# A score pair, the weighted sum, the other score pair: another order of TensorE's work in each unit of an attention kernel

## The chip, the cores and the metric

One NeuronCore of a Trainium2 chip runs the whole kernel. The metric is the device time of one execution in microseconds (us), as the median of several runs. PE is TensorE, ACT ScalarE, DVE VectorE, POOL GpSimd, SP the engine that issues the DMAs.

## The reference

A block of adaptive layer norm, differential attention and a ternary feed-forward product, for four sequences of 2048 tokens with 256 features. There are 16 heads, each with two softmax maps over a head size of 8:

```python
h = _layernorm(x, axis=-1) * (1 + ca) + sa
# attention of h
q, k = h Wq, h Wk     as 32 half-heads of 8;   v = h Wv  as 16 heads of 16
attn_w = softmax(q k^T * 8 ** -0.5)
aw = attn_w[:, :, 0] - lam * attn_w[:, :, 1]
attn = aw v;  attn = attn * rsqrt(mean(attn ** 2) + 1e-5) * subln_w * (1 - LAMBDA_INIT)
x = x + ga * (attn Wo)
h = _layernorm(x, axis=-1) * (1 + cb) + sb
x = x + gb * (h (ternary(Wf) * scale))
```

The scores are 4 x 32 matrices of 2048 x 2048, and each entry goes through an exponential once.

## The kernel before

**Tiling.** The batches b run from 0 to 3 (B = 4). A batch has 8 groups of two heads; two groups make a body, so there are 4 bodies per batch (index `gp`) and 16 in all. A body has 128 units (`BODY`). A unit is one group, one chunk of 512 queries and one block of 128 keys. Sixteen units with the same queries are a segment.

**Score pairs.** `scores(body, u, n)` (L670) makes one score pair: two bf16 matmuls of 64 rows by 128 columns with 512 moving columns, one on the upper and one on the lower half of the array, both at a time, into two PSUM banks. There are three such slots of two banks (`SLOTS`), used in turn; score pair n waits until the exponential of pair n - 3 is done (`exp_done`). Each unit has two score pairs, 2u and 2u + 1.

**Exponentials.** ACT takes the pairs in order (L576): one activation of 128 x 1024 elements from PSUM to `probs`, a ring of four units.

**Weighted sum.** `weighted(body, u)` (L680) multiplies the exponentials of a unit with the values: four float32 matmuls of 128 x 32 side by side with 512 columns, accumulated in the bank `pv` over the 16 units of a segment. It is made two units late (`LAG`). It waits for the exponentials of its own unit, and in the first unit of a segment also for `pv_read`: DVE must have transposed the last segment's sum out of `pv` (L948). DVE then finishes the segment (`segment`, L941), with POOL's power function in the middle (L549).

**Steps.** Into the units are woven the projections of the next batch (steps 0 to 7: two of transpositions, L596, then queries, keys and values, L610 and L602, in the bodies of batches 0 to 2) and the outputs of the batch before (steps 8 to 13: two of the product with Wo, two of transpositions, two of the feed-forward product, in the bodies of batches 1 to 3). Each step is cut into four pieces of float32 matmuls on tiles of 128 x 32, with 256 columns (in all 8 matmuls a piece in the trace) or, for transpositions, 128. A table places them: of the 16 units of a segment, the pieces stand in units 3 to 6 and 11 to 14 (step 0 in 7 to 10):

```python
STEP_PIECES = {NB * (n // 2) + ((7 if n == 0 else 3), 11)[n % 2] + p: (n, p)
               for n in range(A_STEPS + E_STEPS) for p in range(PIECES)}
```

The first piece of step 0 waits for DVE's normed tile (`a_normed`, L825), whose statistics DVE starts behind the last segment of the body before. In the last body of batches 0 to 2, eleven units also carry a part of the maxima that shift the exponentials (`m_step`, L652).

**Order.** Everything on PE stands in one hand-written loop over the units (L747). Each engine runs its own list in order; a wait holds up what stands behind it on that engine.

Of the kernel before, what the change touches and what calls it, by code (L numbers as in the profile page):

```python
# [15 lines left out]
def wait_alone(eng, sem, value, passed):  # L16

    eng.wait_ge(sem, value)
    eng.sem_inc(passed, 1)  # L20
# [17 lines left out]
def adaln_diff_attention(nc, x, wqT, wkT, wvT, woT, lq1, lk1, lq2, lk2, subln, wfT, cT, wmod, out):  # L38
# [11 lines left out]
    PAIRS = 2  # L50
# [60 lines left out]
    with ExitStack() as ctx:  # L111
# [95 lines left out]
        def slot_of(body, n):  # L207
            return (body * 2 * BODY + n) % SLOTS
# [371 lines left out]
        def _(pe):  # L580
# [89 lines left out]
            def scores(body, u, n):  # L670

                buf, tc, blk = u // UNITS, u // NB % NC, u % NB
                pe.wait_ge(exp_done, body * (2 * BODY) + n + 1)
                for half in range(2):
                    at = 64 * half
                    last = nc.tensor.matmul(slots[slot_of(body, n)][:, half, :], keys[buf][at:at + KS_ROWS, n % PAIRS, blk * P:(blk + 1) * P],  # L676
                                            queries[buf][at:at + KS_ROWS, n % PAIRS, tc * CH:(tc + 1) * CH], start=True, stop=True)
                last.then_inc(scores_ready, 1)

            def weighted(body, u):  # L680

                buf, blk, seg = u // UNITS, u % NB, u // NB
                if blk == 0:
                    pe.wait_ge(pv_read, body * SEGS + seg + 1)
                pe.wait_ge(exp_done, SLOTS + body * (2 * BODY) + PAIRS * (u + 1))
                for pair in range(PAIRS):
                    for half in range(2):
                        j = 32 * (2 * pair + half)
                        last = nc.tensor.matmul(pv[j:j + VW, :], values[buf][:, blk, half, :], probs[:, u % PRING, pair, half, :],  # L689
                                                start=(blk == 0), stop=(blk == NB - 1))  # L690
                last.then_inc(pv_done, 1)
# [19 lines left out]
            for b in range(B):  # L711
                pe.wait_ge(m_flag_set, b + 1)
                exact = pe.value_load(m_flag[0:1, 0:1], min_val=0, max_val=1)
                pe.reg_mov(behind, 1)
                with pe.If(exact > 0):

                    if b > 0:
                        for u in range(BODY - LAG, BODY):
                            weighted(b * GP - 1, u)
                    pe.reg_mov(behind, 0)  # L720

                    runs = pe.snap(exact_runs, min_val=0, max_val=B - 1)
                    pe.wait_ge(m_evacuated, (b + 1) * M_STEPS)
                    pe.wait_ge(pv_read, b * (GP * SEGS) + 1)
                    with pe.Fori(0, NG) as g:
                        pe.wait_ge(m_rows_loaded, (runs * EXACT_LOADS + (g + 1) * ROW_LOADS) * DMA)
                        for n in range(4 * NB):
                            head, blk = n // NB, n % NB
                            pair, at = head // 2, 64 * (head % 2)
                            pe.wait_ge(m_reduced, (runs * NG + g) * (4 * NB) + n + 1)  # L730
                            for k in range(NC):
                                last = nc.tensor.matmul(ps[:, 4 * (n % 2) + k, :], queries[0][at:at + KQ, pair, blk * P:(blk + 1) * P],
                                                        keys[0][at:at + KQ, pair, k * CH:(k + 1) * CH], start=True, stop=True)
                            last.then_inc(m_scores, 1)
                    wait_alone(pe, m_reduced, (runs + 1) * NG * (4 * NB) + 2, pe_passed)
                    for k in range(NC):
                        if k > 0:
                            pe.wait_ge(exact_evacuated, runs * NC + k)
                        m_transposes(k).then_inc(exact_product, 1)
                    wait_alone(pe, exact_evacuated, (runs + 1) * NC, pe_passed)  # L740
                    wait_alone(pe, m_rows_loaded, (runs + 1) * (EXACT_LOADS * DMA), pe_passed)
                    pe.reg_add(exact_runs, exact_runs, 1)

                for gp in range(GP):
                    body = b * GP + gp
                    steps, outputs, maxima = b < B - 1, b > 0, b < B - 1 and gp == GP - 1
                    for u in range(BODY):  # L747
                        if u % UNITS == 0:
                            buf = u // UNITS
                            pe.wait_ge(group_loaded[buf], (body + 1) * (GROUP_LOADS * DMA))  # L750
                        for n in (PAIRS * u, PAIRS * u + 1):
                            scores(body, u, n)
                        if u >= LAG:
                            weighted(body, u - LAG)
                        elif gp > 0:
                            weighted(body - 1, BODY - LAG + u)
                        elif b > 0:
                            with pe.If(pe.snap(behind, min_val=0, max_val=1) > 0):
                                weighted(body - 1, BODY - LAG + u)
                        before = aux_before(b, gp, u, steps, outputs, maxima)  # L760
                        if maxima and u in M_UNITS:
                            i = M_UNITS[u]
                            if before[0] == "a":
                                pe.wait_ge(a_evacuated, (body + NC) * A_STEPS + before[1] + 1)
                            elif before[0] == "e":
                                pe.wait_ge(e_evacuated, (body - GP) * E_STEPS + before[1] + 1)
                            if i > 0:
                                pe.wait_ge(m_evacuated, (b + 1) * M_STEPS + i)
                            m_step(b + 1, i)
                        if u in STEP_PIECES:  # L770
                            n, p = STEP_PIECES[u]
                            if (steps if n < A_STEPS else outputs):
                                if p == 0 and before is not None:
                                    if before[0] == "a":
                                        pe.wait_ge(a_evacuated, (body + NC) * A_STEPS + before[1] + 1)
                                    elif before[0] == "e":
                                        pe.wait_ge(e_evacuated, (body - GP) * E_STEPS + before[1] + 1)
                                    else:
                                        pe.wait_ge(m_evacuated, (b + 1) * M_STEPS + before[1] + 1)
                                if n < A_STEPS:  # L780
                                    if n == 0 and p == 0:
                                        pe.wait_ge(a_normed, body + NC + 1)
                                    elif n == 2 and p == 0:
                                        pe.wait_ge(a_evacuated, (body + NC) * A_STEPS + 2)
                                    last = a_piece(n, p, aux)
                                    if p == PIECES - 1:
                                        last.then_inc(a_product, 1)
                                else:
                                    i = n - A_STEPS
                                    if i == 0 and p == 0:  # L790
                                        pe.wait_ge(e_evacuated, (body - GP) * E_STEPS)
                                        pe.wait_ge(e_loaded, (body - GP + 1) * 3 * DMA)
                                    elif i == 2 and p == 0:
                                        pe.wait_ge(e_normed, body - GP + 1)
                                    elif i == 4 and p == 0:
                                        pe.wait_ge(e_evacuated, (body - GP) * E_STEPS + 4)
                                    last = e_piece(i, p, aux)
                                    if p == PIECES - 1:
                                        last.then_inc(e_product, 1)
# [316 lines left out]
```

## Time and profile before

| | us |
|---|---|
| median of 3 runs (lowest, highest) | 4042.49 (4041.13, 4048.74) |
| the profiled execution | 4045.13 |
| its span, first to last instruction | 4043.3 |
| ACT busy | 3783.7 (94%) |
| PE busy | 3753.5 (93%) |
| DVE busy | 1197.4 (30%) |
| POOL busy | 634.0 (16%) |

A busy share is the time in which the engine has at least one instruction in work, over the span. Matmuls overlap in PE's pipeline and their ends are modelled, so PE's pace is better read from the distances between starts than from busy time.
### The profile page before, as it was taken

The numbers are of one execution on the slowest core, as the hardware profiler recorded it, in microseconds if no ns is written. First come the engines' busy times: TensorE is split into PE (matmuls) and PEld (weight loads), VectorE is DVE, ScalarE is ACT, GpSimd is POOL, SyncE is SP. The second block draws the span as 40 slices with busy tenths as digits, with TensorE's granted clock in tenths as the row PEclk, the third lists the DMA queues.
The fourth block names the chain that finished last, engine by engine and source line by source line (L and its number), as shares of the span: only waits on it lengthen the run. The fifth ranks groups of instructions, "written<-read, shape, count | busy, mean of one in ns | idle before, by whom it ended". The sixth has DMA issues, their size and how long they took to land.

```text
span 4043.3 us, 75625 instructions
## 1 busy us (share of the span) xinstructions
PE 3753.5 (93%) x32082; PEld 919.2 (23%) x32082; DVE 1197.4 (30%) x2826; ACT 3783.7 (94%) x4132; POOL 634.0 (16%) x401
## 2 busy tenths in 40 slices
PE   6699999999999999999989999999999999999996
PEld 3121212222122222222222222222221212222123
DVE  7322222223332322323423223232331212212124
ACT  1599999999999999999989999999999999999992
POOL 4111212111120210202012121211211010101000
PEclk8799999999999999999999999999999999999998
DMA  3302112210231313113130221313012121201202
GB/s 125 88 25 36 41 34 36 37 36 25 34 54 35 53 32 48 39 35 50 35 56 25 40 49 35 54 35 49 29 34 38 24 40 16 49 3 30 35 13 62
DMA packets 112430, 163.26 MB, mean 40 GB/s; under 512 B 18820, under 2 KB 86660, under 8 KB 111880
## 3 DMA queue, kind: packets, MB, share of 16 engines
q1 hardware_dynamic: 112072, 158.19, 20.6%
q8 instruction: 261, 4.28, 0.5%
q14 instruction: 97, 0.79, 0.1%
HBM read 97.82 MB, written 60.32 MB: 39 GB/s over the span
## 4 chain that ended last, share of the span: by engine, by line
ACT 62%; issue 19%; PE 11%; DVE 5%; POOL 2%; SPq 1%; DMA 1%; DVEq 0%; POOLq 0%; ACTq 0%
ACT probs L576 61%; PE ps L689 5%; PE ps L676 3%; PE ps L602 1%; DVE stats L814 1%; POOL seg_rs L549 1%; DVE normed L825 1%; PE ps L596 1%; DVE seg_t L948 1%; POOL a_rest L522 0%; POOL a_parts L524 0%; SPq L316 0%; POOL e_rstd L529 0%; DVE e_tmp L934 0%; DMA m_scr<-wmod_sb 0%
## 5 line engine op out<-in xcount | busy, mean ns | idle before, releaser
L576 ACT ACTIVATE probs<-ps 128x1024 f32<-128x1024 f32 x4096 | 3763.0, 1291 | 87.6 <-PE ps L676 86.0
L689 PE MATMUL ps<-probs,values 128*32 128x512 f32 x16384 | 2193.3, 607 | 26.3 <-DVE seg_t L948 16.9
L676 PE MATMUL ps<-queries,keys 64*128 64x512 bf16 x8192 | 1441.9, 386 | 152.6 <-DMA queries<-m_scr 24.7
L549 POOL TENSOR_TENSOR seg_rs<-seg_ms,neg_half 64x16 f32<-64x16 f32 x128 | 370.2, 2892 | 2582.1 <-DVE seg_ms L957 2582.1
L676 PEld LDWEIGHTS ps<-queries,keys 64*128 64x128 bf16 x8192 | 339.1, 93 | 1868.6 <-ACT probs L576 1723.2
L689 PEld LDWEIGHTS ps<-probs,values 128*32 128x32 f32 x16384 | 322.9, 108 | 654.3 <-issue 569.3
L948 DVE STREAM_TRANSPOSE seg_t<-ps 128x512 f32<-128x512 f32 x128 | 91.7, 716 | 1126.1 <-PE ps L689 1126.1
L959 DVE TENSOR_TENSOR seg_n<-seg_d,seg_rs 64x256 f32<-64x256 f32 x128 | 53.4, 417 | 386.2 <-POOL seg_rs L549 386.2
L596 PE MATMUL ps<-ident,normed 128*32 128x128 f32 x2048 | 103.0, 300 | 64.4 <-DVE normed L825 44.6
L910 DVE TENSOR_SCALAR a_qk<-ps 128x512 f32<-128x512 f32 x64 | 44.2, 691 | 331.6 <-PE ps L610 331.3
L934 DVE TENSOR_TENSOR e_tmp<-ps,e_gate 128x512 f32<-128x512 f32 x64 | 44.2, 691 | 330.3 <-PE ps L602 330.2
L596 PEld LDWEIGHTS ps<-ident,normed 128*32 128x32 f32 x2048 | 70.1, 121 | 192.4 <-issue 131.5
L963 DVE SCALAR_TENSOR_TENSOR seg_a<-seg_n,subln_sb 32x256 f32<-32x256 f32 x256 | 105.7, 413 | 6.0
L610 PE MATMUL ps<-a_hT,w_q 128*32 128x256 f32 x1024 | 81.3, 415 | 11.8 <-DVE a_hT L908 11.8
L512 POOL CAST a_parts<-a_qk 128x512 bf16<-128x512 f32 x48 | 34.5, 719 | 359.5 <-DVE a_qk L910 359.5
L967 DVE STREAM_TRANSPOSE seg_o<-seg_a 32x512 f32<-32x512 f32 x128 | 89.5, 700 | 4.4
L908 DVE TENSOR_SCALAR a_hT<-ps,a_cols 128x512 f32<-128x512 f32 x32 | 25.6, 808 | 183.0 <-PE ps L596 183.0
L602 PE MATMUL ps<-w_f,e_hT 128*32 128x256 f32 x1024 | 75.8, 389 | 0.9 <-DVE e_hT L931 0.9
L602 PE MATMUL ps<-w_o,e_attn 128*32 128x256 f32 x1024 | 75.1, 386 | 0.0
L602 PE MATMUL ps<-w_v,a_hT 128*32 128x256 f32 x1024 | 73.5, 379 | 0.0
L610 PE MATMUL ps<-a_hT,w_k 128*32 128x256 f32 x1024 | 73.5, 379 | 0.0
L931 DVE TENSOR_SCALAR e_hT<-ps,e_cols 128x512 f32<-128x512 f32 x32 | 25.9, 810 | 157.6 <-PE ps L596 157.6
(118 smaller groups left out, 1203.2 us busy)
## 6 DMA issues: line engine op xcount, KB each, us to landing
queries<-q_scr SPq DMA_DIRECT2D x384, 64.0 KB
keys<-k_scr SPq DMA_DIRECT2D x384, 64.0 KB
v_scr<-a_v SPq DMA_DIRECT2D x128, 128.0 KB, 2.0
values<-v_scr SPq DMA_DIRECT2D x32, 512.0 KB
q_scr<-a_parts SPq DMA_DIRECT2D x32, 384.0 KB, 2.6
k_scr<-a_parts SPq DMA_DIRECT2D x32, 384.0 KB, 2.5
a_x<-in_x_dram SPq DMA_DIRECT2D x16, 512.0 KB, 4.6
attn_scr<-seg_o SPq DMA_DIRECT2D x128, 64.0 KB, 1.6
```

Source lines behind the costliest of these rows:

```text
L549: nc.gpsimd.tensor_tensor(seg_rs[:, :], seg_ms[:, :], neg_half[0:64, :], ALU.pow).then_inc(seg_rs_done, 1)
L576: nc.scalar.activation(probs[:, u % PRING, n % PAIRS, :, :], slots[slot_of(body, n)], ACT.Exp).then_inc(exp_done, 1)
L596: last = nc.tensor.matmul(bank[j:j + 32, n * P:(n + 1) * P], src[:, n, c * P + j:c * P + j + 32], ident[:, :], start=True, stop=True)
L602: last = nc.tensor.matmul(bank[j:j + 32, (n % 2) * E:(n % 2 + 1) * E], hT[:, c, n * P + j:n * P + j + 32], w[:, c, :], start=(c == 0), sto ...
L610: last = nc.tensor.matmul(bank[j:j + 32, t], w[:, c, f * P + j:f * P + j + 32], hT[:, c, t], start=(c == 0), stop=(c == EC - 1))
L676: last = nc.tensor.matmul(slots[slot_of(body, n)][:, half, :], keys[buf][at:at + KS_ROWS, n % PAIRS, blk * P:(blk + 1) * P], queries[buf][ ...
L689: last = nc.tensor.matmul(pv[j:j + VW, :], values[buf][:, blk, half, :], probs[:, u % PRING, pair, half, :], start=(blk == 0), stop=(blk = ...
L910: last = V.tensor_scalar(a_qk[:, i - 2, :], bank, SCALING if i < 4 else 1.0, None, ALU.mult)
L948: V.transpose(seg_t[:, :, :].rearrange("p c d -> p (c d)"), pv).then_inc(pv_read, 1)
L959: V.tensor_tensor(seg_n[:, :, :], seg_d[:, :, :], seg_rs[:, :].rearrange("p (c o) -> p c o", o=1).broadcast_to([64, NQ, VD]), ALU.mult).th ...
L963: last = V.scalar_tensor_tensor(seg_a[:, :, h * VD:(h + 1) * VD], seg_n[q, :, :], 1.0 - LAMBDA_INIT, subln_sb[q, :].rearrange("p (o d) -> ...
L967: V.transpose(seg_o[:, :], seg_a[:, :, :].rearrange("p c d -> p (c d)")).then_inc(seg_done, 1)
```

## The change

In each unit PE now makes score pair 2u, then the weighted sum of two units ago, then score pair 2u + 1, and then the step's piece or the part of the maxima. Until now both score pairs stood ahead of the weighted sum. No instruction is added or taken away, the waits stay with their instructions, and no other engine's list changes.

```diff
@@ -748,8 +748,7 @@
                         if u % UNITS == 0:
                             buf = u // UNITS
                             pe.wait_ge(group_loaded[buf], (body + 1) * (GROUP_LOADS * DMA))
-                        for n in (PAIRS * u, PAIRS * u + 1):
-                            scores(body, u, n)
+                        scores(body, u, PAIRS * u)
                         if u >= LAG:
                             weighted(body, u - LAG)
                         elif gp > 0:
@@ -757,6 +756,7 @@
                         elif b > 0:
                             with pe.If(pe.snap(behind, min_val=0, max_val=1) > 0):
                                 weighted(body - 1, BODY - LAG + u)
+                        scores(body, u, PAIRS * u + 1)
                         before = aux_before(b, gp, u, steps, outputs, maxima)
                         if maxima and u in M_UNITS:
                             i = M_UNITS[u]
```

PE at the start of body 0, before: L676 are score matmuls (two for a pair), L689 those of the weighted sum.

```order
L676 MATMUL ps<-queries,keys 128x512 x12
L689 MATMUL ps<-probs,values 32x512 x4
L676 MATMUL ps<-queries,keys 128x512 x4
L689 MATMUL ps<-probs,values 32x512 x4
L676 MATMUL ps<-queries,keys 128x512 x4
```

The same place now:

```order
L676 MATMUL ps<-queries,keys 128x512 x10
L689 MATMUL ps<-probs,values 32x512 x4
L676 MATMUL ps<-queries,keys 128x512 x4
L689 MATMUL ps<-probs,values 32x512 x4
L676 MATMUL ps<-queries,keys 128x512 x4
```

The first weighted sum stands behind five score pairs instead of six. In units without a piece the sequence is otherwise the same, two pairs and a sum in turn.

PE around the last two pieces of step 9 in a body with outputs (units 77 to 82), before: L602 with w_o is the piece.

```order
L602 MATMUL ps<-w_o,e_attn 32x256 x4
L676 MATMUL ps<-queries,keys 128x512 x4
L689 MATMUL ps<-probs,values 32x512 x4
L602 MATMUL ps<-w_o,e_attn 32x256 x4
L676 MATMUL ps<-queries,keys 128x512 x4
L689 MATMUL ps<-probs,values 32x512 x4
L676 MATMUL ps<-queries,keys 128x512 x4
L689 MATMUL ps<-probs,values 32x512 x4
```

The same place now:

```order
L602 MATMUL ps<-w_o,e_attn 32x256 x4
L676 MATMUL ps<-queries,keys 128x512 x2
L689 MATMUL ps<-probs,values 32x512 x4
L676 MATMUL ps<-queries,keys 128x512 x2
L602 MATMUL ps<-w_o,e_attn 32x256 x4
L676 MATMUL ps<-queries,keys 128x512 x2
L689 MATMUL ps<-probs,values 32x512 x4
L676 MATMUL ps<-queries,keys 128x512 x4
L689 MATMUL ps<-probs,values 32x512 x4
L676 MATMUL ps<-queries,keys 128x512 x4
```

In units with a piece the two pairs, until now four matmuls in a row, stand apart, one ahead of the sum and one between sum and piece.

## Rows read from the trace of the kernel before

**Rows 1.** The page: engines' busy time, and two of the costliest groups.

```profile
PE 3753.5 (93%) x32082; PEld 919.2 (23%) x32082; DVE 1197.4 (30%) x2826; ACT 3783.7 (94%) x4132; POOL 634.0 (16%) x401
...
L576 ACT ACTIVATE probs<-ps 128x1024 f32<-128x1024 f32 x4096 | 3763.0, 1291 | 87.6 <-PE ps L676 86.0
...
L676 PE MATMUL ps<-queries,keys 64*128 64x512 bf16 x8192 | 1441.9, 386 | 152.6 <-DMA queries<-m_scr 24.7
```

**Rows 2.** Timeline of ACT (start, length, instruction, count, idle before): three runs.

```profile
400.94 234.77 ACT L576 ACTIVATE probs<-ps 128x1024 f32<-128x1024 f32 x256 [1.72 <-PE ps L676]
...
3413.08 234.77 ACT L576 ACTIVATE probs<-ps 128x1024 f32<-128x1024 f32 x256 [0.41 <-PE ps L676]
...
3883.45 82.61 ACT L576 ACTIVATE probs<-ps 128x1024 f32<-128x1024 f32 x90 [0.41 <-PE ps L676]
```

**Rows 3.** Timeline of PE, last piece of step 2 in body 5.

```profile
1385.13 1.07 PE L689 MATMUL ps<-probs,values 128*32 128x512 f32 x8
1386.01 0.61 PE L610 MATMUL ps<-a_hT,w_q 128*32 128x256 f32 x8
1386.56 0.61 PE L676 MATMUL ps<-queries,keys 64*128 64x512 bf16 x4
1387.09 1.07 PE L689 MATMUL ps<-probs,values 128*32 128x512 f32 x8
1388.09 0.60 PE L676 MATMUL ps<-queries,keys 64*128 64x512 bf16 x4
1388.62 1.06 PE L689 MATMUL ps<-probs,values 128*32 128x512 f32 x8
```

**Rows 4.** Timeline of PE in that step; middle row: the second pair alone.

```profile
1380.66 0.61 PE L676 MATMUL ps<-queries,keys 64*128 64x512 bf16 x4
...
1380.89 0.38 PE L676 MATMUL ps<-queries,keys 64*128 64x512 bf16 x2
...
1381.19 1.06 PE L689 MATMUL ps<-probs,values 128*32 128x512 f32 x8
```

**Rows 5.** Timeline of PE, a piece of transpositions in body 1.

```profile
401.93 0.40 PE L596 MATMUL ps<-ident,normed 128*32 128x128 f32 x8
402.27 0.60 PE L676 MATMUL ps<-queries,keys 64*128 64x512 bf16 x4
```

**Rows 6.** Timelines at body 0's start and in body 1; L576's durations (ns least/median/most).

```profile
149.07 5.61 ACT L576 ACTIVATE probs<-ps 128x1024 f32<-128x1024 f32 x6 [33.59 <-PE ps L676]
...
150.15 0.61 PE L676 MATMUL ps<-queries,keys 64*128 64x512 bf16 x2 [0.27 <-ACT probs L576]
...
400.51 0.61 PE L676 MATMUL ps<-queries,keys 64*128 64x512 bf16 x4
...
L576 ACT ACTIVATE probs<-ps x4096: 1017/1167/1863, 149.1 to 3964.6; 128x1024 f32<-128x1024 f32 x196
```

**Rows 7.** Timeline of ACT: the exponential behind the last piece of rows 3.

```profile
1386.99 1.03 ACT L576 ACTIVATE probs<-ps 128x1024 f32<-128x1024 f32 x1
```

**Rows 8.** Timeline of PE across a segment's start.

```profile
2000.74 0.39 PE L676 MATMUL ps<-queries,keys 64*128 64x512 bf16 x2
2001.06 1.06 PE L689 MATMUL ps<-probs,values 128*32 128x512 f32 x8
...
2003.04 1.06 PE L689 MATMUL ps<-probs,values 128*32 128x512 f32 x8
```

**Rows 9.** Timeline of PE: unit 7 of body 5, and unit 82 of body 4.

```profile
1357.23 0.42 PE L596 MATMUL ps<-ident,normed 128*32 128x128 f32 x8 [2.24 <-DVE normed L825]
...
1257.60 1.06 PE L689 MATMUL ps<-probs,values 128*32 128x512 f32 x8 [1.29 <-DVE seg_t L948]
```

**Rows 10.** Timeline of PE in body 7, units with a part of the maxima.

```profile
1925.64 0.60 PE L676 MATMUL ps<-queries,keys 64*128 64x512 bf16 x4
...
1927.71 0.60 PE L676 MATMUL ps<-queries,keys 64*128 64x512 bf16 x4
```

**Rows 11.** Timeline of PE: the weighted sum at the start of batch 1.

```profile
1098.86 1.93 PE L689 MATMUL ps<-probs,values 128*32 128x512 f32 x8
```

## The prediction

> **What bounds the kernel now.** I read the page first. ACT is busy for 3783.7 us of a span of 4043.3, and 3763.0 of that is one line, the 4096 exponentials of L576; PE is busy for 3753.5 us [rows 1]. Both shares are above 90%, so the page alone doesn't say which engine sets the pace. The timeline of ACT does: from 150 to 3966 us its exponentials stand in a few long runs without a gap, 256 in 234.77 us, which is 0.917 us each, and a run ends mostly where a body of 128 units begins [rows 2]. One unit (two exponentials) takes ACT 2 x 0.917 = 1.83 us. All the idle time in front of L576 is 87.6 us [rows 1], 33.6 of it before the first one [rows 6]. So ACT bounds the kernel, there are some 55 us to gain at most, and the question is how far PE is from taking the lead.
>
> **PE's unit, from the distances between starts.** I call a score pair S, the weighted sum W, a step's piece P. In the step of rows 3 the starts give W to P 0.88, P to S 0.55, the two S and then W 0.53, and W to S, where no piece stands between, 1.00. Of the 0.53 the second S takes 0.22 to 0.23 and S to W 0.30 to 0.32 [rows 4, 8]; I split it 0.22 and 0.31. So a unit with a piece of 256 columns takes PE 0.22 + 0.31 + 0.88 + 0.55 = 1.96 us, 0.13 more than ACT, and a unit without a piece 0.22 + 0.31 + 1.00 = 1.53. A piece of transpositions (128 columns) has P to S 0.34 [rows 5]: 1.75. PE is thus slower than ACT in four units of a 256-column step and catches up in the four after it.
>
> **How late a score pair may be.** S may start 0.06 after the exponential three before it has ended (the first exponential starts at 149.07 and lasts at least 1.02, the fourth pair starts at 150.15), and its own exponential ends at the earliest 0.43 + 1.02 = 1.45 after S starts (S at 400.51, its exponential at 400.94) [rows 2, 6]. In the kernel before, S of the next unit starts 0.31 + 0.88 + 0.55 = 1.74 after the second S was released, and its exponential must end 4 x 0.917 - 0.06 = 3.61 after that point. The first has 3.61 - 1.74 - 1.45 = 0.42 to spare, the fourth 0.42 - 3 x 0.13 = 0.03. The trace has just that: an exponential that is fed in time lasts longer than the least, as it is begun before the one ahead has ended, and the exponential behind the fourth piece lasts 1.03 us, against a least of 1.02 [rows 6, 7]. The old order is within hundredths of a microsecond of stalling ACT, with no stall. This check is why I trust the working.
>
> **What the change does in a unit without a piece.** The sequence S S W S S W is the same, only W belongs to the units otherwise: it comes one pair, 0.92 us, earlier, and the S that is late behind it is the second of a unit instead of the first. PE's time and what is to spare stay as they are.
>
> **What it does in a unit with a piece.** S S W P becomes S W S P. The joints W to P (0.88) and S to S (0.22) go; W to S (1.00) and S to P come. W to S alone is 0.12 more than W to P. No row shows S to P. P has the operand type, the 128x32 tiles and the weights' shape of W, so the nearest row is S to W, 0.31 [rows 4]. The low end is S to S, 0.22 [rows 4]: what S takes where its like follows. The high end is 0.39, the mean length of an S matmul on the page [rows 1]: P starts when S has ended. I take 0.31. The unit is then 0.31 + 1.00 + 0.31 + 0.55 = 2.16 (to a hundredth, as the parts are rounded), which is 0.20 more than before; with a transposition piece 1.95.
>
> The Trainium skill (TensorEngine Tiling, Key Properties) says that a change of tiling mode, not of tile alone, drains TensorE; S is on 64x128 and W and P on 128x32, so the new order has four changes in such a unit where the old had two. Its sense agrees with the joints above. By its price for a matmul that nothing overlaps (TensorE: Matmul & The Clock Gate, Single matmul latency), an estimate of 0.38 us for 512 columns, S to P would be at the high end, while the row S to W doesn't pay that much; the sum would be that of rival B.
>
> **The sum.** In the new order the second S is the late one: released S, W, S puts it 0.31 + 1.00 = 1.31 after the first S was released, and its exponential must end at 3.61. To spare: 3.61 - 1.31 - 1.45 = 0.85.
> - A 256-column step overruns by 4 x (2.16 - 1.83) = 1.31, less 0.85 = 0.46 us of ACT idle. The four units behind it give back 4 x 0.30, enough for the 0.85. There are 6 such steps in each of the 12 bodies with steps and 4 in each of the 12 with outputs: 120 x 0.46 = 55.2.
> - 48 of them (steps 2, 4, 6 and 8, three units into a segment) come right behind a W that waits for DVE's transposition. There W follows W after 1.98 instead of 1.83 (2001.06 and 2003.04, [rows 8]), so 0.1 of what was to spare is gone: 4.8.
> - A transposition step overruns by 4 x 0.12 = 0.46 and stays within 0.85. Step 10 starts right behind the wait of unit 82 (below), with less to spare: 12 x 0.16 = 1.9.
> - Unit 7 of 11 bodies: P waits for DVE's normed tile, 2.24 us (at 1357.23, [rows 9]). DVE starts that behind the W of unit 1, which now comes one exponential earlier: -0.92. But behind the stall the second S waits for W: 1.31 - 0.92 = +0.39, and the seven units to the end of step 1 overrun by 0.12 each with nothing to spare, +0.81. 11 x 0.29 = 3.2.
> - Unit 82 of the 12 bodies with outputs: W waits 1.29 for the segment's transposition (at 1257.60), which DVE makes behind the outputs' layer norm [rows 9]. Behind W now stands an S that is due one exponential sooner, +0.92, less the 0.33 that ACT has lost just before, after step 9's last piece: 12 x 0.57 = 6.8.
> - Units with a piece of the maxima take 2.07 already (1925.64 to 1927.71, [rows 10]) and lie right before a step in 9 cases; those four units find nothing to spare and the step costs about 1.1 instead of 0.46: 9 x 0.65 = 5.9.
> - At the start of batches 1 to 3, PE's branch and a slow W (1.93 against 1.06, [rows 3, 11]) now stand before the second S: about 0.45 more each, 1.4.
>
> Sum 79 us. PE hides nothing of it, since it is PE that is late. The profiled execution took 4045.1 us with what lies around its span, which is 2.6 above the median of 4042.5: 4124.3 there, **4122** for the median. DVE, POOL and the DMA queues run the same instructions and none gets near a bound.
>
> **Rivals.**
> - **A, P follows S at streaming pace** (0.22). The unit is 2.08, a step overruns by 0.98 - 0.85 = 0.12: 120 x 0.12 = 14, and with the other terms (5, 8, 4 and 1, less 5 at unit 7) +27: 4070. For it: W's own matmuls follow at such a pace. Against: S to W, the same change of shape, costs 0.31. 7%.
> - **B, P waits for S to end** (0.39). The unit is 2.24, a step costs 4 x 0.41 - 0.85 = 0.79: 95 us, and 31 for the rest: +126, 4168. For it: S would stand alone between two of the other shape, which no row shows. Against: the same row S to W. 8%.
> - **C, faster.** If an S alone costs only its stream, W to S drops by 0.09 to 0.91 as well and the unit is 0.31 + 0.91 + 0.22 + 0.55 = 1.99. The point is 1.83 + 0.85 / 4 = 2.05: under it no step stalls ACT. The earlier W then brings the 0.92 at unit 7 in full, 11 x 0.92 = 10, and PE may be spared the slow W behind that stall (in some bodies 1.2 us more on ACT, 8 to 11 in all); unit 82 takes 7 back. About -12: 4030. Against: W to S is 1.00 in every plain unit. 3%.
> - **D, nothing.** The change would do nothing if a score pair could be later than I reckon, 1.31 instead of 0.85, so that the step's overrun is covered. Then the small terms stay, against the 10 at unit 7: about 4045. Against: the fourth piece of the old order leaves just the 0.01 to 0.03 that the working says. 4%.
>
> **Numbers.** The forecast has 78%. Its own spread is that of S to P between 0.29 and 0.33 (6 us for each 0.01) and of a few slow W more or less: 4105 to 4138. For 8 in 10 I take 4090 to 4145, which cuts into A and B from both sides; the bounds of the unknown joint, 4070 and 4168, lie outside because the row S to W is so near a kin. About 0.2% (8 us) is what can be told from no change. Faster 3% (C), same 4% (D), slower 93%.
>
> **What would show it.** In a 256-column step PE's units are 2.16 us long, with S to P 0.31 and W to S 1.00. ACT's runs break inside each such step, two gaps of 0.1 to 0.35 before odd exponentials; step 0's stall is shorter by 0.9. If S to P is 0.22 or 0.39, rivals A and B have it. I am wrong in kind if PE's unit is 2.16 and ACT still shows no gap, or if W to S, with a piece behind that S, is no longer 1.00.

## The result, and the profile after

| | before | after |
|---|---|---|
| median (lowest, highest), us | 4045.6 (4041.1, 4048.8) | 4148.6 (4142.9, 4158.9) |
| profiled execution / its span | 4045.1 / 4043.3 | 4142.9 / 4141.1 |
| ACT busy / PE busy | 3783.7 / 3753.5 | 3821.4 / 3862.0 |

The ratio is 1.026 (95% interval 1.0247 to 1.0273): 103 us slower. I had forecast slower by 79, with 4145 as the upper end. The sign came out and so did where the time is lost, the size was a quarter too small, and the time lies 3.6 us outside the range.

The page after, to set beside [rows 1]: busy times, the chain by engine, the exponentials and the score matmuls.

```profile
PE 3862.0 (93%) x32082; PEld 877.5 (21%) x32082; DVE 1194.6 (29%) x2826; ACT 3821.4 (92%) x4132; POOL 634.6 (15%) x401
...
PE 51%; ACT 28%; issue 12%; DVE 6%; POOL 2%; SPq 1%; DMA 1%; DVEq 0%; POOLq 0%; ACTq 0%
...
L576 ACT ACTIVATE probs<-ps 128x1024 f32<-128x1024 f32 x4096 | 3800.7, 1253 | 152.7 <-PE ps L676 146.2
...
L676 PE MATMUL ps<-queries,keys 64*128 64x512 bf16 x8192 | 1513.7, 387 | 123.5 <-DMA queries<-m_scr 21.4
```

The same instructions, no more of them, and yet PE is busy for 108 us more. The chain that ended last, which was ACT for 62% and PE for 11% of the span, now runs through PE for half of the span.

Timeline of ACT in body 5 after, from the end of step 2 to unit 82 (start, length, count, idle before). Before, the same exponentials stood in one run, the last row.

```profile
1410.59 1.94 ACT L576 ACTIVATE probs<-ps 128x1024 f32<-128x1024 f32 x2 [0.27 <-PE ps L676]
1412.80 12.94 ACT L576 ACTIVATE probs<-ps 128x1024 f32<-128x1024 f32 x14 [0.27 <-PE ps L676]
1425.91 1.94 ACT L576 ACTIVATE probs<-ps 128x1024 f32<-128x1024 f32 x2 [0.18 <-PE ps L676]
1428.12 12.96 ACT L576 ACTIVATE probs<-ps 128x1024 f32<-128x1024 f32 x14 [0.27 <-PE ps L676]
1441.36 1.94 ACT L576 ACTIVATE probs<-ps 128x1024 f32<-128x1024 f32 x2 [0.27 <-PE ps L676]
...
1518.19 1.94 ACT L576 ACTIVATE probs<-ps 128x1024 f32<-128x1024 f32 x2 [0.18 <-PE ps L676]
1520.40 5.61 ACT L576 ACTIVATE probs<-ps 128x1024 f32<-128x1024 f32 x6 [0.27 <-PE ps L676]
1526.95 3.77 ACT L576 ACTIVATE probs<-ps 128x1024 f32<-128x1024 f32 x4 [0.94 <-PE ps L676]
```

```profile
1361.33 135.77 ACT L576 ACTIVATE probs<-ps 128x1024 f32<-128x1024 f32 x148 [1.16 <-PE ps L676]
```

Each 256-column step makes two gaps, before and after a pair of exponentials, 16 exponentials apart from the next step's. From 1410.59 to 1518.19 there are seven such stretches, 15.37 us on average.

How long sixteen take in the kernel before, and how long if ACT never waits, can be read from four rows of its timeline, each at the start of a window. The first is 65 exponentials of body 0 in units that have no step in that body, the second the last two of them, the third 16 of body 5 from behind the last piece of step 2 on, the fourth the one behind the last piece of step 3.

```profile
267.10 59.71 ACT L576 ACTIVATE probs<-ps 128x1024 f32<-128x1024 f32 x65
...
324.07 2.75 ACT L576 ACTIVATE probs<-ps 128x1024 f32<-128x1024 f32 x2
...
1386.99 14.78 ACT L576 ACTIVATE probs<-ps 128x1024 f32<-128x1024 f32 x16
...
1401.65 1.04 ACT L576 ACTIVATE probs<-ps 128x1024 f32<-128x1024 f32 x1
```

Without a step, 63 starts take 324.07 - 267.10 = 56.97 us, which is 0.904 us each and 14.46 for sixteen. With a step they took 14.66 already in the kernel before. So a 256-column step cost ACT 0.20 us in the old order and costs 0.91 in the new one, 0.71 more. The rows hide the old 0.20. An exponential that comes late is begun behind the end of the one ahead instead of before it, 1.04 us after its start instead of 0.904; but the idle time between the two is then 0.02, too little to break a run.

PE in the last unit of step 2 and the plain ones behind it, after (for [rows 3]):

```profile
1409.16 1.06 PE L689 MATMUL ps<-probs,values 128*32 128x512 f32 x8
1410.16 0.39 PE L676 MATMUL ps<-queries,keys 64*128 64x512 bf16 x2
1410.47 0.64 PE L610 MATMUL ps<-a_hT,w_q 128*32 128x256 f32 x8
1411.05 0.39 PE L676 MATMUL ps<-queries,keys 64*128 64x512 bf16 x2
1411.37 1.06 PE L689 MATMUL ps<-probs,values 128*32 128x512 f32 x8
1412.36 0.61 PE L676 MATMUL ps<-queries,keys 64*128 64x512 bf16 x4
1412.90 1.06 PE L689 MATMUL ps<-probs,values 128*32 128x512 f32 x8
```

W to W is 2.21 us, where it was 1.96 and the forecast said 2.16. W to S is 1.00 as forecast, S to P 0.31 to 0.32, but P to S is 0.57 to 0.58 instead of 0.55: the piece itself is reported with 0.64 instead of 0.61. The plain unit behind it is 1.53 as ever.

### The profile page after: what moved, and what is told of

The parts are those of the page before. It is cut to its first block, busy times and chain, and to the rows that moved or that the text cites. A ratio compares the mean times of both kernels' runs of the same rounds, so it can differ in the third digit from the quotient of the medians.

```text
span 4141.1 us, 75625 instructions
## 1 busy us (share of the span) xinstructions
PE 3862.0 (93%) x32082; PEld 877.5 (21%) x32082; DVE 1194.6 (29%) x2826; ACT 3821.4 (92%) x4132; POOL 634.6 (15%) x401
## 4 chain that ended last, share of the span: by engine, by line
PE 51%; ACT 28%; issue 12%; DVE 6%; POOL 2%; SPq 1%; DMA 1%; DVEq 0%; POOLq 0%; ACTq 0%
ACT probs L576 28%; PE ps L689 26%; PE ps L676 16%; PE ps L602 4%; PE ps L610 3%; PE ps L596 2%; DVE seg_t L948 1%; DVE stats L814 1%; DVE normed L825 1%; POOL seg_rs L549 1%; POOL a_rest L522 0%; POOL a_parts L524 0%; SPq L316 0%; POOL e_rstd L529 0%; DVE e_tmp L934 0%
## 5 line engine op out<-in xcount | busy, mean ns | idle before, releaser
L576 ACT ACTIVATE probs<-ps 128x1024 f32<-128x1024 f32 x4096 | 3800.7, 1253 | 152.7 <-PE ps L676 146.2
L689 PE MATMUL ps<-probs,values 128*32 128x512 f32 x16384 | 2192.4, 607 | 48.4 <-DVE seg_t L948 43.5
L676 PE MATMUL ps<-queries,keys 64*128 64x512 bf16 x8192 | 1513.7, 387 | 123.5 <-DMA queries<-m_scr 21.4
L676 PEld LDWEIGHTS ps<-queries,keys 64*128 64x128 bf16 x8192 | 367.2, 93 | 2351.1 <-ACT probs L576 2151.9
L689 PEld LDWEIGHTS ps<-probs,values 128*32 128x32 f32 x16384 | 322.7, 108 | 597.3 <-issue 416.0
L602 PE MATMUL ps<-w_o,e_attn 128*32 128x256 f32 x1024 | 77.6, 396 | 0.0
L602 PE MATMUL ps<-w_f,e_hT 128*32 128x256 f32 x1024 | 76.0, 388 | 0.9 <-DVE e_hT L931 0.9
L602 PE MATMUL ps<-w_v,a_hT 128*32 128x256 f32 x1024 | 75.9, 388 | 0.0
L913 DVE COPY a_v<-ps 128x256 f32<-128x256 f32 x64 | 23.8, 419 | 177.8 <-PE ps L602 177.0
```

The costliest lines, as they stand in the source:

```text
L576: nc.scalar.activation(probs[:, u % PRING, n % PAIRS, :, :], slots[slot_of(body, n)], ACT.Exp).then_inc(exp_done, 1)
L602: last = nc.tensor.matmul(bank[j:j + 32, (n % 2) * E:(n % 2 + 1) * E], hT[:, c, n * P + j:n * P + j + 32], w[:, c, :], start=(c == 0), sto ...
```

## The experiments

Theory T: each unit with a piece has two more changes of tile shape on PE, that costs PE 0.24 us there, and what a step adds beyond what PE has to spare (0.85 us in the forecast) stalls ACT. Rival R: the cost is in the place of the second score pair, which comes due too soon behind the weighted sum. The kernel before ran beside each group: 4046.1 us beside e1 to e4, 4044.4 beside e5 to e7, 4043.3 beside e8.

**e1: S, W, P, S.** The second pair moves behind the piece, in all units.

```diff
-                        scores(body, u, PAIRS * u + 1)
                         before = aux_before(b, gp, u, steps, outputs, maxima)
...
                                     last = e_piece(i, p, aux)
                                     if p == PIECES - 1:
                                         last.then_inc(e_product, 1)
+                        scores(body, u, PAIRS * u + 1)
```

> Every unit is S, W, P, S: the second score pair stands behind the sum and the piece. Theory T (the time went into two more changes of tile shape in each unit with a piece): the joints are again S to W, W to P, P to S, S to S, the unit takes 1.96 us, and the second S has 3.61 - (0.31 + 0.88 + 0.55) - 1.45 = 0.42 us to spare, as the first had in the old order; no step stalls ACT: 4045, within 8 us of the kernel before, and W to S and P to S as before. Rival R (it is the place: a score pair behind the weighted sum is due too soon, whatever the joints): the second S now has the sum and the piece ahead of it, at least as much as in the change, so 4150 or more.

4048.9 us, ratio 1.0007 (0.9998 to 1.0016). The second pair now stands behind the sum and the piece, as far back as it can, and the whole loss is gone (the 2.8 us that are left can't be told from none). Its PE timeline at the last piece of step 2:

```profile
1402.43 1.07 PE L689 MATMUL ps<-probs,values 128*32 128x512 f32 x8
1403.31 0.61 PE L610 MATMUL ps<-a_hT,w_q 128*32 128x256 f32 x8
1403.86 0.61 PE L676 MATMUL ps<-queries,keys 64*128 64x512 bf16 x4
1404.39 1.06 PE L689 MATMUL ps<-probs,values 128*32 128x512 f32 x8
```

W to W is 1.96 again. R as it was put falls: being behind the sum doesn't cost by itself, and the loss goes with the two added joints. Where the place does cost, e3 shows.

**e2: the new order only in units with a piece or a part of the maxima.** Two lines around the loop's second score pair; `late` says whether it comes behind the sum.

```diff
                         scores(body, u, PAIRS * u)
+                        late = (u in STEP_PIECES and (steps if STEP_PIECES[u][0] < A_STEPS else outputs) or maxima and u in M_UNITS)
+                        if not late:
+                            scores(body, u, PAIRS * u + 1)
...
-                        scores(body, u, PAIRS * u + 1)
+                        if late:
+                            scores(body, u, PAIRS * u + 1)
```

> S, W, S, P only in units with a piece or a part of the maxima, the old order in all others. T: the same 672 units take 0.24 us more of PE as in the change, and nothing is won back elsewhere; at the seams between the two orders a sum comes one pair sooner or later, which costs a little more: +105 to +125, 4150 to 4170. R, if the place in the plain units carries a part of the cost: clearly less than the change's +103, in proportion to the 672 of 2048 units, some +35.

4168.5 us, 1.0301 (1.0286 to 1.0315), +122. A third of the units carries more than the whole loss. The surplus of about 20 us over the change has a part that the expectation left out: units 127, 0 and 1 keep the old order here, so the first piece of step 0 waits 2.43 us for DVE (at 1393.99) where in the change it waits 1.92, and e7 below shows what that place is worth. The rest, seams between two orders among it, wasn't taken apart.

**e3: the new order only in units without a piece.** As e2 with `late = not (...)`.

> S, W, S only in units without a piece, the old order in units with one. T: no joint is added anywhere. But at each step's end a sum comes one pair sooner just when the score pairs have nothing to spare: S of the next unit has 0.03 to spare and the second S behind the sum is 1.31 - 0.92 = 0.39 later than that, so 0.36 a step behind 256-column steps (120) and less elsewhere: +30 to +45, 4075 to 4090, with PE's unit in steps still 1.96. R: the plain units are two thirds of all units, so two thirds of +103: +70, 4115.

4085.3 us, 1.0093 (1.0077 to 1.0108), +39. PE's unit in steps is the old one (W at 1405.96, next W at 1407.92). ACT has one gap a step, where the old order gives way to the new one. ACT's timeline in step 2 to 4:

```profile
1399.98 14.78 ACT L576 ACTIVATE probs<-ps 128x1024 f32<-128x1024 f32 x16 [0.28 <-PE ps L676]
1415.03 14.77 ACT L576 ACTIVATE probs<-ps 128x1024 f32<-128x1024 f32 x16 [0.28 <-PE ps L676]
```

Starts 15.05 apart instead of 14.66: 0.39, against 0.36 in the working. By the starts of the exponentials in the trace, the 120 steps take 44 us more than before, unit 82 and the step behind it 8, and unit 7 takes 15 less, as in e7; the +39 is what is left of these and some small parts. No joint was added here, so a sum that comes one pair sooner does cost, but only where nothing is left to spare. This is what is right in R.

**e4: the new order only in the first two pieces of each step.** As e2 with `late = ... and STEP_PIECES[u][1] < 2`, without the maxima.

> S, W, S, P in the first two pieces of each step, the old order in the last two. Half of the added PE time of the change. T with a fixed amount to spare per step (0.85 us): the step overruns by 2 x 0.37 + 2 x 0.13 = 1.0 us instead of 1.5, of which what is beyond the spare counts; with the seams counted, +35 to +45: 4080 to 4090. If each added joint cost its time on its own, with no cover: half of +103, +52 or more.

4092.3 us, 1.0116 (1.0101 to 1.0132), +46. That lies 1 us above T's interval and 6 below half of the change's loss, with seams in it. The time doesn't tell the two apart by itself. The trace does more: sixteen exponentials with a 256-column step in them take 0.26 us more than before on average, where PE's joints add 2 x 0.24 = 0.49. In the change they take 0.71 more for 4 x 0.24 = 0.98. So 0.23 of the added time is covered in one and 0.27 in the other: about the same amount, not the same share, as T has it.

**e5 and e6: PE's time by itself, old and new order.** Exponentials of the first 256 of each 512 queries only. This leaves out half of the exponentials, so that ACT never sets the pace; the rest of the ring holds ones.

```diff
-                    nc.scalar.activation(probs[:, u % PRING, n % PAIRS, :, :], slots[slot_of(body, n)], ACT.Exp).then_inc(exp_done, 1)
+                    nc.scalar.activation(probs[:, u % PRING, n % PAIRS, :, 0:CH // 2], slots[slot_of(body, n)][:, :, 0:CH // 2], ACT.Exp).then_inc(exp_done, 1)
...
+            link.then(V.memset(probs[:, :, :, :, :], 1.0))
```

> The kernel before with exponentials of only the first 256 of each 512 queries (the rest of the ring is filled once with ones), so ACT takes about half as long and PE sets the pace everywhere: PE's own time for the old order. T: 672 units with a piece at 1.96 or 1.75 us and 1376 without at 1.53 give 3.39 ms for the units, with start, end and waits on DVE about 3610 to 3680 us in all.

> The changed kernel with the same half exponentials: PE's own time for the new order. T: 672 x 0.244 = 164 us more than the same with the old order (0.244 as the distances between starts in the changed kernel's trace give it: unit 2.207 against 1.963), between 150 and 175. R: no difference beyond 10 us, since PE's work would be the same and only the deadlines of the score pairs moved.

3801.2 us (3799.6 to 3803.6) with the old order, 3965.4 (3961.3 to 3972.5) with the new: 164 us apart, where the expectation had 672 x 0.244 = 164; with runs that spread over 4 and 11 us the match to the microsecond is luck. The pages of the two, old order first:

```profile
L576 ACT ACTIVATE probs<-ps 128x512 f32<-128x512 f32 x4096 | 2222.7, 595 | 1375.1 <-PE ps L676 1375.1
```

```profile
L576 ACT ACTIVATE probs<-ps 128x512 f32<-128x512 f32 x4096 | 2300.0, 595 | 1467.6 <-PE ps L676 1453.7
```

ACT is idle for over a third of the time in both, so no score pair's due time matters, and the difference is PE's alone. The change thus adds 164 us to PE and 103 to the kernel: 61 us of it are covered by what PE has to spare beside ACT. This sum doesn't show how the cover lies over the steps; the traces of e4 and of the change do. The level of e5 I missed: 3801 where I had put 3610 to 3680. The units' 3.39 ms stand, but I had put PE's waits too low. The trace of e5 has PE waiting 63.9 us for DVE's transpositions of the sum and 58.1 for the normed tiles; the rest I didn't follow up.

**e7: the new order only in units 127, 0 and 1 of each body.** As e2 with `late = u in (0, 1, BODY - 1)`.

> The new order only in units 127, 0 and 1 of each body, which carry no piece. T: no joint is added; the last weighted sum of a body comes one exponential sooner, DVE starts the statistics for step 0 sooner, and the wait of the first piece in unit 7 (11 bodies) is shorter by 0.9 us: 1.83 becomes 0.91 us of ACT idle each, 10 us in all, 4035. If the sum's place doesn't set DVE's start: no change.

4028.3 us, 0.9964 (0.9951 to 0.9978): 16 us faster than the kernel before, the best of all. PE at unit 7 of body 5, for the first of [rows 9]:

```profile
1348.85 1.07 PE L689 MATMUL ps<-probs,values 128*32 128x512 f32 x8
1351.23 0.43 PE L596 MATMUL ps<-ident,normed 128*32 128x128 f32 x8 [1.31 <-DVE normed L829]
1351.59 0.60 PE L676 MATMUL ps<-queries,keys 64*128 64x512 bf16 x4
1352.12 1.06 PE L689 MATMUL ps<-probs,values 128*32 128x512 f32 x8
```

PE waits 1.31 us for DVE instead of 2.24, 0.93 less, in 11 bodies: the 10 us. The rest comes behind it. Two windows, granted clock in the third field from the right; first the kernel before, behind that wait, then e7 at the same place:

```profile
1358.50:1360.50 2.00, 2.00 (x18) 0.59 (x16) 0.00 (x0) 1.67 (x2) 0.00 (x0) 0.50 0.52 68
```

```profile
1352.50:1354.50 2.00, 2.00 (x28) 0.66 (x24) 0.00 (x0) 2.00 (x3) 0.00 (x0) 1.00 0.52 61
```

After 2.24 us without a matmul PE goes at a granted 0.50 (1.2 GHz) here; after 1.31 it stays at 1.00 (2.4 GHz). Not every wait is followed by this. Of the nine bodies with steps that don't start a batch, the granted clock falls to 0.50 within 5 us behind the wait in six of the kernel before (2.24 us), in three of the change (1.92) and in none of e7 (1.31). The 1.2 us of ACT that such a stretch costs (the [1.16] at 1361.33 above) are gone in e7. ACT has other gaps there in two bodies, 0.91 and 0.59 us some 26 us behind unit 7, the first with the clock at 1.00; what makes them stays open.

**e8: S, S, P, W.** The old order with the weighted sum moved behind the piece.

```diff
-                        if u >= LAG:
-                            weighted(body, u - LAG)
...
                                     last = e_piece(i, p, aux)
                                     if p == PIECES - 1:
                                         last.then_inc(e_product, 1)
+                        if u >= LAG:
+                            weighted(body, u - LAG)
```

> S, S, P, W: the piece stands ahead of the weighted sum, behind both score pairs. T: two changes of tile shape as in the old order (S to P, W to S), so the unit of a 256-column step stays within 0.03 us of 1.96 although P again stands behind S. In unit 7 of 11 bodies the weighted sum now waits behind the piece that waits for DVE, 0.9 us more ACT idle each: +10, 4055. The trace also tells what the two missing parts of the prediction belong to: if S to P is 0.31 here and 0.32 in the change, 0.01 belongs to a score pair that stands alone; if the piece is again stretched by 0.02 when it comes behind S, that belongs to the change of shape. Rival: if S to P is dear for itself, the unit is 2.05 or more and the time 4090.

4051.7 us, 1.0020 (1.0011 to 1.0029), +8, with a spread of 4041.7 to 4057.2; the profiled execution is the fastest of the eleven. The +10 of the expectation is met in part by luck. On its page PE waits 55.0 us for the normed tiles, 10 more than before (44.6), but 6.5 for DVE's transpositions of the sum, 10 less than before (16.9): the wait of the sum at unit 82 is gone, which the expectation didn't have. Its PE timeline in step 2:

```profile
1382.59 0.61 PE L676 MATMUL ps<-queries,keys 64*128 64x512 bf16 x4
1383.13 0.64 PE L610 MATMUL ps<-a_hT,w_q 128*32 128x256 f32 x8
1383.59 1.04 PE L689 MATMUL ps<-probs,values 128*32 128x512 f32 x8
1384.56 0.60 PE L676 MATMUL ps<-queries,keys 64*128 64x512 bf16 x4
```

The unit is 1.97 (1382.59 to 1384.56). P stands behind S, as in the change, and is reported with the same 0.64; W stands behind P and has 1.04, not its 1.06 or 1.07. So the stretch of 0.02 to 0.03 us falls on whichever of the two comes first behind S. S and P are 0.54 - 0.23 = 0.31 apart, where in the change, with one pair alone ahead, they are 0.31 to 0.32. The rows round this away, the starts in the traces resolve it: the median over the 480 such units is 0.309 here and 0.319 in the change, and in e6 S to W is 0.309 behind two pairs and 0.320 behind a lone one. A hundredth belongs to the pair that stands alone.

## Why the prediction was right and where it was wrong

**ACT bounds the kernel and PE is at its heels: right. ACT's pace, and "with no stall": wrong.** PE's unit before, 1.96, and a few hundredths to spare behind a fourth piece were what the whole forecast hung on. But the 0.917 is a mean over steps that already stall ACT, 0.20 us each; where nothing holds it up, ACT takes 0.904 an exponential and 1.81 a unit. The exponential of 1.03 us behind the fourth piece, which I took for one fed just in time, was one that came late. Put through the same working, 0.904 gives a stall of 0.11 behind a step of the old order (0.37 to spare, less 3 x 0.16), where 0.20 was measured, and 0.81 in the new one with its real unit (4 x 0.40 less 0.80), where 0.91 was measured. Both miss by a tenth, so their difference comes out at 0.70. With 0.917 and the real unit it is 0.65 in the new order and none in the old, nearly the same difference: the check that I trusted agreed by luck, and the step's sum is hardly hurt by it. The transposition pieces are: their units overrun ACT by 2.00 - 1.81 = 0.19, where I had 0.12. (The runs of [rows 2] begin behind units 7 and 82, not where a body begins; and 0.92 less 0.33 is 0.59, not 0.57.)

The working gave e1 and e8 (0 and +10 expected, +3 and +8 measured), e2 and e3 came within their ranges (+105 to +125 and +30 to +45, measured +122 and +39), e2 with the 0.24 that had been read from the changed kernel. e4 lay 1 us above its range, e5 over 100 above, and e7 gained 16 us where 10 were expected.

**Plain units unchanged: right as long as the order is the same throughout** (1.53 in the rows after). e3 shows the limit: a seam costs 0.39 us behind a step.

**W to S 1.00 in the new place: right.** **S to P 0.31 from the row S to W: nearly right** (0.319).

**The step that failed is P to S.** I wrote "P to S 0.55" over from the old order, where P stands behind W and meets no change of shape. In the new order P comes first behind S and takes the stretch that W carries in every row: P to S is 0.57 to 0.58. No row of before had a piece first behind S, so the bounds should have been put on the piece's own length too, not on the joint ahead of it alone. P to S is 0.025 of the miss and the hundredths at the two joints behind a lone pair are the other 0.019: the unit is 2.21, not 2.16. That is small, but the forecast itself said that a hundredth is worth 6 us, because there is nothing to spare: 0.044 (2.207 in e6's expectation less 2.163, the forecast's sum with its parts to a thousandth) x 100 x 6 = 26 us, and 103 - 79 = 24 were missing.

Term by term it is less neat. Between its first and its last exponential ACT takes 106 us more in the trace of the change than in that of the kernel before:

| | in the sum | in the traces |
|---|---|---|
| 120 steps of 256 columns, those behind the maxima among them | 55.2 + 4.8 + 5.9 | 85 |
| unit 82 and step 10 behind it | 6.8 + 1.9 | 13 |
| unit 7 with steps 0 and 1, and the starts of batches | 3.2 + 1.4 | 7 |

Step 11 and small differences make up the rest. The traces' spans differ by 98, because the set-up ahead of the first exponential was 6.5 us shorter in the profiled execution of the change (142.5 us against 149.1) and the end behind the last one 1.9 shorter. The change doesn't touch the set-up, and in the traces of the other runs with whole exponentials the first one starts anywhere from 144.4 to 152.1.

**The range was too narrow.** I bounded one joint and let the others stand as certain. The unit had four joints with new neighbours, and each hundredth of any of them moved the result by 6 us. The spread of 4105 to 4138 covered two or three hundredths of one joint only.

**The small terms.** Unit 82: the sum waits 1.82 us there after (1525.52) instead of 1.29, and the gap of ACT is 0.94 instead of 0.41 (1526.95 after, 1259.03 before): 0.53 against 0.57. The step behind it, with transposition pieces, cost 0.5 where I had 0.16. Unit 7: P waits less, 1.92 instead of 2.24, and ACT stands idle for 0.81 and then 0.29 us where it was 1.93 and then 1.16; the shift of 0.92 by the earlier sum is shown by itself in e7. The 28 exponentials that follow in one row take 26.91 us, 1.5 more than at 0.904 apart: there the transposition units overrun. In body 9, where neither trace has the stretch at half clock, all this comes to +0.79 and not to the forecast's +0.29. Over the nine bodies that don't start a batch it was 3 us all the same, because the change has the slow stretch in three of them and the kernel before in six: luck.

PE in unit 7 of body 5 and at unit 82, after:

```profile
1381.31 0.42 PE L596 MATMUL ps<-ident,normed 128*32 128x128 f32 x8 [1.92 <-DVE normed L825]
...
1525.52 1.06 PE L689 MATMUL ps<-probs,values 128*32 128x512 f32 x8 [1.82 <-DVE seg_t L948]
```

ACT behind unit 7 of body 5, after:

```profile
1382.10 1.02 ACT L576 ACTIVATE probs<-ps 128x1024 f32<-128x1024 f32 x1 [0.81 <-PE ps L676]
1383.41 26.91 ACT L576 ACTIVATE probs<-ps 128x1024 f32<-128x1024 f32 x28 [0.29 <-PE ps L676]
```

**The rivals.** A and B rested on S to P at 0.22 or 0.39; it is 0.31 to 0.32. C and D needed a unit below 2.05 or more to spare; the unit is 2.21. C's one true part, that an earlier sum frees DVE sooner and can spare PE the slow stretch, is worth 16 us where it comes without new joints (e7).

**What stays open.** A score pair differs from a sum or a piece in its tiles, its operand type and its weights. Which of these makes a joint between the two kinds dear wasn't separated: "change of tile shape" names the joint, not a shown cause. Nor was the tenth of a microsecond found by which both stalls exceed the working.

## What to carry to other kernels

Count the changes from one kind of matmul to the other along TensorE's order, not the instructions: two work orders of the same matmuls differed by 0.24 us in each unit where a score pair was put alone between a sum and a piece. Take an engine's own pace from a stretch in which no other engine can hold it up, from start to start; here a long run without a visible gap had stalls of 0.20 us in it. When two engines run within a few per cent of each other, work out how late each hand-over may be, take every duration from a place with the same neighbour in front, and give the range a width by what a hundredth is worth. An order that is bad in the bulk can be good at a seam: try it where the wait stands (here units 127, 0 and 1).

## What the runs showed of the hardware that I had not expected

The first group of 128x32 matmuls behind a score pair is stretched by 0.02 to 0.03 us (0.64 against 0.61 for a piece, 1.06 against 1.04 for a sum), on top of the wider distance from the pair ahead, whichever kind it is. Exponentials of 128x1024 from PSUM start 0.904 us apart when ACT is never kept waiting, though one by itself lasts 1.02. And the granted clock fell to 0.50 behind six of nine waits of PE of 2.24 us, three of nine of 1.92 and none of nine of 1.31, at otherwise the same place.
